# Cross-attention and a gated FFN on one core: the next tile's scores behind its projections, its masks and maxima in the second square layer

## The reference

```python
src, tgt = ctx, layernorm(x)
src_trans = (src @ W_src.T + b_src) * mask[:, :, None]     # 512 -> 2 * 256: K and V
tgt_trans = (tgt @ W_tgt.T + b_tgt) * mask[:, :, None]     # Q
k, v = split(src_trans); q = tgt_trans                     # 8 heads of 32
scores = einsum('bthd,bshd->bhts', q, k) / sqrt(32)
attn = softmax(where(mask[:, None, None, :] == 0, -inf, scores))
tgt_update = einsum('bhts,bshd->bthd', attn, v)
x = x + concat([tgt, tgt_update]) @ W_out.T + b_out
h = layernorm(x)
h = silu(h @ w1.T * s1) * (h @ w2.T * s2)                  # 256 -> 1024
h = gelu(h @ h1.T * t1)                                    # 1024 -> 1024
h = gelu(h @ h2.T * t2)                                    # 1024 -> 1024
out = x + h @ w3.T * s3                                    # 1024 -> 256
```

## Time and profile before

| | |
|---|---|
| median of 3 runs | 996.01 us (994.23 to 997.73) |
| profiled execution | 997.81 us, its span 996.0 us |
| PE busy | 933.2 us (94%), 7716 matmuls |
| DVE busy | 601.4 us (60%) |
| ACT busy | 388.5 us (39%) |
| POOL busy | 72.3 us (7%) |
| DMA | 64.54 MB, mean 65 GB/s |
| mean granted TensorE clock | 0.982 |

### The profile page before, as it was taken

One profiled execution on the slowest core, in us unless ns is written; L12 is line 12 of the kernel. 1 busy time (PEld: TensorE's weight loads), 2 busy tenths in 40 slices (PEclk: granted clock), 3 DMA queues, 4 the chain that ended last, 5 costly groups with the idle time before them and its releaser, 6 DMA issues.

```text
span 996.0 us, 20724 instructions
## 1 busy us (share of the span) xinstructions
PE 933.2 (94%) x7716; PEld 887.0 (89%) x7716; DVE 601.4 (60%) x1151; ACT 388.5 (39%) x1073; POOL 72.3 (7%) x96
## 2 busy tenths in 40 slices
PE   5757999999999999999999999999999999998998
PEld 5546989989899998989999898999989899998898
DVE  5584475674847567484756748475584846547352
ACT  4343243353434335343432525244252524425231
POOL 2261000101000010100001010000100000000000
PEclk9778999999999999999999999999999999999999
DMA  8802103030120302113030210303021030202000
GB/s 319 348 1 90 34 12 112 22 102 20 51 81 11 111 21 90 31 36 95 11 111 21 90 32 20 111 11 111 21 85 36 11 115 17 84 12 64 22 12 12
DMA packets 51437, 64.54 MB, mean 65 GB/s; under 512 B 6736, under 2 KB 43984, under 8 KB 51408
## 3 DMA queue, kind: packets, MB, share of 16 engines
q1 hardware_dynamic: 51408, 64.15, 19.4%
HBM read 44.21 MB, written 19.92 MB: 64 GB/s over the span
## 4 chain that ended last, share of the span: by engine, by line
PE 83%; DVE 7%; issue 5%; DMA 1%; ACT 1%; SPq 1%; POOL 0%; DVEq 0%; ACTq 0%
PE F L519 49%; PE F L593 6%; PE G L503 6%; PE G L386 5%; PE G L519 5%; PE G L409 5%; PE G L398 3%; DVE g L964 3%; DVE mx L879 2%; PE S L424 2%; PE G L486 1%; PE G L511 1%; DMA p_dram<-pb 1%; ACT pr L716 1%; DMA WK<-wk 1%
## 5 line engine op out<-in xcount | busy, mean ns | idle before, releaser
L519 PE MATMUL F<-hAh,H 128*128 128x256 f32 x1024 | 247.4, 286 | 7.6 <-DVE hAl L985 3.8
L519 PE MATMUL F<-hBh,H 128*128 128x256 f32 x1024 | 244.8, 283 | 0.8 <-DVE hBl L985 0.8
L519 PE MATMUL F<-hAl,H 128*128 128x256 f32 x1024 | 243.7, 281 | 0.0
L696 ACT ACTIVATE g<-F,scols 128x256 f32<-128x256 f32 x256 | 107.3, 470 | 342.1 <-PE F L519 341.9
L519 PE MATMUL F<-hBl,H 128*128 128x256 f32 x1024 | 240.6, 279 | 0.0
L519 PEld LDWEIGHTS F<-hAh,H 128*128 128x128 f32 x1024 | 195.0, 190 | 9.7 <-DVE hAl L985 4.6
L519 PEld LDWEIGHTS F<-hAl,H 128*128 128x128 f32 x1024 | 195.9, 191 | 0.3
L519 PEld LDWEIGHTS F<-hBl,H 128*128 128x128 f32 x1024 | 193.3, 189 | 0.4
L519 PEld LDWEIGHTS F<-hBh,H 128*128 128x128 f32 x1024 | 191.8, 187 | 1.4 <-DVE hBl L985 1.0
L716 ACT ACTIVATE pr<-pr,nmx 128x128 f32<-128x128 f32 x256 | 99.1, 388 | 44.8 <-DVE nmx L883 44.6
L983 DVE CAST hAh<-g 128x512 fp32r<-128x512 f32 x128 | 55.8, 436 | 93.3 <-ACT g L696 92.2
(11 more groups left out here) (118 smaller groups left out, 1438.5 us busy)
## 6 DMA issues: line engine op xcount, KB each, us to landing
p_dram<-pb SPq DMA_DIRECT2D x30, 512.0 KB, 3.5
pr<-p_dram SPq DMA_DIRECT2D x120, 128.0 KB, 2.6
H_raw<-h SPq DMA_DIRECT2D x16, 512.0 KB, 13.8
cT<-ctx_t SPq DMA_DIRECT2D x15, 512.0 KB, 3.5
out<-y SPq DMA_DIRECT2D x32, 128.0 KB, 1.7
x_in<-x_t SPq DMA_DIRECT2D x15, 256.0 KB, 2.7
W_raw<-w SPq DMA_DIRECT2D x6, 512.0 KB, 9.4
mrow<-mask_row SPq DMA_DIRECT2D x15, 128.0 KB, 3.3
```

Of the source, the lines that this page charges most:

```text
L519: return mm(bank, W[0][:, k, cols], part[:, k, :], start=first, stop=last)
L696: fn(g[:, q % 2, m, :], F[q % 2][:, m, :], ACT.Gelu, scale=scols[:, col:col + 1]).then_inc(gelu_ready, 1)
```

## The change

On PE, `scores(a)` is taken from the start of the gates, and `scores(n)` is put behind V of tile n, the last of the projections. On DVE, the masks and maxima of tile a go from the gates and the projections, and those of tile n are put into the second square layer: `mask_scores(n, 0)` and `row_max(n, 0)` behind the split of q=7, `mask_scores(n, 1)` behind `x2_lo`, `row_max(n, 1)` behind the split of q=11. Nothing is added or removed; each runs one step earlier in the sequence. Step 0, which runs the scores, masks and maxima of tile 1 itself, keeps them and gets those of tile 2 as well. Step 14 has none any more.

```diff
--- before.py
+++ after.py
@@ -597,8 +597,6 @@
             def gates_part(f, a, n, general):
 
                 first = isinstance(f, int) and f == 0
-                if a is not None and not first:
-                    scores(a)
                 for q in range(4):
                     gate_up(f, q, general)
                 if first:
@@ -611,6 +609,7 @@
                     project_k(n, 1)
                     project_q(n)
                     project_v(n)
+                    scores(n)
 
             def middle_part(f, a, general):
 
@@ -1013,8 +1012,6 @@
 
                 first = isinstance(f, int) and f == 0
                 keep_residual(f)
-                if a is not None and not first:
-                    mask_scores(a, 0)
                 if first:
                     ln1_stats(2)
                 gate_times_up(f, 0)
@@ -1022,8 +1019,6 @@
                 gate_times_up(f, 1)
                 split(f, 1)
                 gate_times_up(f, 2)
-                if a is not None and not first:
-                    row_max(a, 0)
                 if first:
                     ln1_apply(2)
                     look(17)
@@ -1037,17 +1032,14 @@
                     bias_mask_q(1)
                     mask_scores(1, 0)
                     row_max(1, 0)
-                if a is not None:
-                    mask_scores(a, 1)
                 if first:
+                    mask_scores(1, 1)
                     row_max(1, 1)
                     bias_v(1)
                     for c in on_dve[6:]:
                         look(c)
                 if n is not None:
                     bias_mask_k(n)
-                if a is not None and not first:
-                    row_max(a, 1)
                 if n is not None:
                     mask_bias(n)
                     bias_mask_q(n)
@@ -1065,6 +1057,9 @@
                     turn_blocks(a, 1)
                 for q in range(4, 8):
                     split(f, q)
+                if n is not None:
+                    mask_scores(n, 0)
+                    row_max(n, 0)
                 if a is not None:
                     residual_ln2_stats(a)
                     ln2_apply(a)
@@ -1072,11 +1067,15 @@
                 split(f, 9)
                 if a is not None:
                     x2_lo(a)
+                if n is not None:
+                    mask_scores(n, 1)
                 split(f, 10)
                 if m is not None:
                     ln1_stats(m)
                     ln1_apply(m)
                 split(f, 11)
+                if n is not None:
+                    row_max(n, 1)
                 scale_out(f, 0)
                 scale_out(f, 1)
                 add_residual(f, 0)
```

## The result

| | before | changed |
|---|---|---|
| median of 5 runs | 996.26 us (994.23 to 998.87) | 987.31 us (986.39 to 989.96) |
| ratio, 95% interval | | 0.9914 (0.9889 to 0.9939) |
| profiled execution | 997.81 us, span 996.0 | 986.39 us, span 984.6 |

That is faster as forecast, but 981.1 us had been forecast and a gain of 14.9; the measured time is inside the range by 0.2 us only, at the end that had been set for the drain rival. From the one profiled execution to the other it is 11.4 us. The profile before lies 1.6 above its median, and the one after is the lowest of its five runs.

What follows compares the result with a forecast made beforehand. PE, busy 933.2 of 996.0 us, was taken as the bound. Terms: 11.5 + 0.7 + 3.75 - 1.02 = 14.9 us, giving 982.9 against the profiled 997.81 and 981.1 against the median 996.01; range 977.0 to 987.5.

Steps and rivals of the forecast that it cites:

- drain rival: At the moved scores: the tiling-mode drain travels along, so the move on PE nets nothing; 984.6 us, chance 0.16.
- Term 1: Tiles f=1 to 12: K's wait for DVE's last gate product falls from 1.29 to 0.60 us, gain 0.69 a tile.
- the rest stays: At K: 0.60 us of wait remains, the last g pair lying behind the last up matmul, covered by four transposes only.
- Term 2: Scores on PE: 1.29 us removed at the gates, 1.02 added behind V, net gain 0.27 a tile for f=1 to 13.
- (a) to (e): Moved masks and maxima on DVE, the scores' need of qT, and the softmax's DRAM trip: all costed at nothing.
- late scaling: Second square layer: row_max(n, 1) pushes output scaling and gates past the slack; 989.4 us, chance 0.06.
- moved, not removed: Steady tiles: both per-tile gains come back as waits elsewhere, tile 14 and tile 0 effects stay; 993.3 us, chance 0.04.
- Term 3: Tile 14, without projections to hide the softmax: attend's second half comes 3.75 us earlier, removed scores included.
- Term 4: Tile 0: tile 2's scores between V and the branch cost between 0 and 1.02 us, taken as 1.02.
- slower rival: Start of every middle layer: narrow matmuls behind the projections drop PE to the lower clock; 999 or 1017 us, chance 0.06.
- The sentence beside it: Step 14: by the skill's rule on idle gaps, the 2.6 us wait at attend may cost 1.4 us more.

Runs made afterwards that it cites:

- max_late: The kernel before with only row_max(a, 0) moved from the gates to behind split(f, 3): 991.06 us, ratio 0.9942.
- early_k_after: The changed kernel with two PE waits relaxed, so K and the transposes no longer wait for q=3's gate products and silus: 974.89 us, ratio 0.9756.
- after_again: The changed kernel unaltered, run again: 987.88 us, ratio 0.9908 to the kernel before.
- before_v: The changed kernel with tile 2's scores, in tile 0 alone, ahead of V instead of behind it: 982.49 us in one execution.
- early_k_before: The kernel before with two PE waits relaxed, so K and the transposes no longer wait for q=3's gate products and silus: 981.84 us, ratio 0.9839.
- at_attend: The changed kernel with the scores directly ahead of attend in the square layers instead of behind V: 982.14 us, ratio 0.9833.
- pe_only: The kernel before with only the scores on PE moved behind V, masks and maxima left in place on DVE: 1019.36 us, ratio 1.0229.
- behind_branch: The changed kernel with tile 2's scores behind the branch on the low bits instead of ahead of it: 986.31 us, ratio 0.9888.

## Why the prediction was right or wrong

**Term 1, right.** K's wait went from 1.29 to 0.50 instead of 0.60, and in step 13 from 0.86 to 0.41. Another 0.06 a tile comes from the gates' matmuls (116.7 ns apart instead of 117.8). That is 0.85 for 0.69. `max_late` shows it to be the maximum alone. What the term took as given, "the rest stays", held for this change but not for the kernel: q=3's product isn't in K's bank, and `early_k_after` takes the rest away.

**Term 2, wrong: "The step from V into the scores I price like the step from V into the middle layer."** It costs 0.28 more: 3.55 us for 3.27. Removed were 1.30 a tile, as forecast, and added were 1.30, not 1.02, so the move on PE nets nothing. This was the drain rival, and the upper end that the term had named. I chose the nearest row by place, one that leads from full-size into full-size matmuls, where the earlier trace rows had what the whole block costs between full-size matmuls, 1.29. The parts differ at the two places: in the gates 0.08 on the way in and 0.10 on the way out, behind V 0.28 on the way in and 0.08 less than before on the way out. So the equal sums, 1.30, are measured, but no single price of a switch gives both, and that they agree is in part luck. The Trainium skill (TensorEngine Tiling (Array Packing), Key Properties) has a change of tiling mode drain the array; the runs agree in direction: 1.30 where the block is entered and left on its own, 1.10 where it shares that with attend. But from the scores' row tiles to attend's column tiles the mode changes too, and there no cost shows. Cost: 0.28 in 13 tiles, 3.6 us.

**A cost that was not in the sum.** In 11 of the 13 tiles the 127 distances between matmuls of the first square layer went from 116.7 to 117.8 ns: 0.15 us a tile, 1.6 in all. So a steady tile is -1.30 + 1.30 - 0.85 + 0.15 = -0.70. It isn't shown to belong to the change: in `after_again`, the same kernel, it is 5 of the 13.

**Costs at nothing, right,** all of (a) to (e). The residual starts directly behind the maximum (462.81), the second mask leaves 1.29 of idle, the scaling starts directly behind the last `nmx` (481.67), and DVE still idles 0.43 ahead of the first `g` after it. `qT` is there at 439.1, the scores come at 441.55. The rival "late scaling" and "moved, not removed" have nothing for them.

**Term 3, right in kind, too small.** Step 14's own part of the difference is -3.56 - 1.30 = -4.9 in the profiled execution, for 3.75 (the 1.30 are the scores added behind V in step 13). The first reciprocal comes 61.07 us behind K of step 13 (898.09) instead of 63.59, 3.8 earlier by the same count, where 3.75 had been forecast. The rest is DMA: the four loads that took SP 3.41 us in step 14 before take 2.52 in this execution and 3.10 in `after_again`. There attend comes 4.0 earlier by this count and waits the 2.6 that I had forecast, but the lower clock behind it takes 1.7 back. The wait of 2.22 at the split is 0.91, and the slow matmuls behind it are gone.

**Term 4, mis-sized: 1.02, measured 2.94** (V's start to the second middle matmul 7.59, then 10.53). I took the upper bound to be the scores' own length, "because no releaser is shown". The scores took 1.11 of it, and the time without a releaser itself grew by 1.82. The bounds lacked a case: that the unseen thing depends on what stands ahead of it. It was a load of code behind the branch, and it started later (`before_v`).

**The sum.** Against the 982.9 forecast for it, the profiled execution of the changed kernel took 3.5 us more. By the terms: 3.6 for term 2, 1.6 for the spacing and 1.9 for term 4, less 2.0 for term 1, less 1.1 for term 3, less 0.4 by which V starts earlier in tile 0 for reasons ahead of the edit: 3.6, for 3.5. That the time came inside the range is partly luck: against 7.1 us of misses in terms 2 and 4 and the spacing stand 3.1 us that terms 1 and 3 gave beyond their forecast, 0.9 of them a shorter DMA. The other 2.7 of the 6.2 between 981.1 and 987.31 lie in the step to the median: I took 1.8 off because the profile before stood that far above its median, and the one after stood 0.9 below its own.

**The clock.** The slower rival didn't come: every steady tile of the changed kernel has a granted clock of 1.00. The sentence beside it did come in some executions: the wait at attend in step 14 brought the output projection to 1.2 GHz in `after_again`, and not in the first profile. The Trainium skill (TensorE: Matmul & The Clock Gate, HAM oscillation) agrees as a direction; which wait is long enough the rows don't settle, see below.

## What to carry to other kernels

When a block is moved on a busy engine, price it by all that it costs where it stands now, the way in and out included, and put it beside another narrow block where there is one: here 1.10 us instead of 1.30. Before reordering work to shorten a wait, check whether what is waited for really holds the resource; one wait on the wrong PSUM bank was worth more than the whole reordering. And move a block on one engine only together with what it feeds on another: PE's half alone cost 22.8 us, through a wait that grew by 0.6 and the clock behind it.

## What the hardware showed that I had not expected

- **Two spacings.** 128x256 matmuls at full clock lie 116.7 or 117.8 ns apart, mostly one value for a whole stretch, with nothing waited for. In the gates the value goes with the order: 117.8 in every step of the three profiles in which the scores stand directly ahead of them (before, `max_late`, `early_k_before`), 116.7 in the other ten, and in step 15, which has no scores, in all. In the first square layer it isn't fixed by the order: 117.8 in none of the 13 stretches before, in 11 after, in 5 of `after_again`, in none of `at_attend` and `early_k_after`. The cause is open.
- **The clock behind short waits.** It fell behind 1.87 us at K in seven tiles of `pe_only` and not behind the same wait in five; it fell behind 2.04 (`behind_branch`), 2.61, 2.70, 2.71 and 2.90 us at attend, and behind 2.2 to 3.5 us at the splits of step 14 (before, `early_k_before`, `pe_only`, `max_late`). It didn't behind 2.37 at attend before, 2.40 (`before_v`), 1.98 (`early_k_before`), 1.76 or less. So the length of the wait alone doesn't decide it.
- **The branch.** 3.2 to 3.7 us of idle on PE behind full-size matmuls, 5.4 to 5.6 behind narrow ones, 0.97 where V starts just ahead of the flag. A 16 KB load of code ends 1.50 to 1.60 us ahead of PE's first instruction in all of them.
